# A two-layer graph network on one core: the edge load of a group of layer 0 is cut into four

## The reference, cut to what matters

```python
e = edge_attr @ W_edge + b_edge                  # 200000 x 128 times 128 x 256
msg = jax.nn.relu(x[src] + e)                    # gather of x rows by the edge's source
agg = jax.ops.segment_sum(msg, dst, num_segments=x.shape[0])
h = (1.0 + eps) * x + agg
h = jax.nn.relu(h @ W1 + b1) @ W2 + b2           # then a norm over the nodes, relu, residual, layernorm
```

## Time and profile before

| what | value |
|---|---|
| median of 3 timed runs | 5319.87 us (5314.68 to 5321.25) |
| profiled execution, its own time | 5282.99 us |
| its span from the first to the last instruction | 5281.1 us |
| layer 0's adds, first and last start | 34.71 us and 2505.15 us |
| mean granted TensorE clock | 0.828 of full speed |

### The profile page before, as it was taken

How to read it: one execution, slowest core, us unless ns; L and a number is a source line. 1 busy time by engine, 2 the same in 40 slices (tenths; PEclk the granted TensorE clock), 3 DMA queues, 4 the chain that set the end, 5 groups by cost and what they waited for, 6 DMA issues and landing times.

```text
span 5281.1 us, 64039 instructions
## 1 busy us (share of the span) xinstructions
PE 4024.7 (76%) x19280; PEld 2795.1 (53%) x19281; DVE 2232.9 (42%) x4481; ACT 719.6 (14%) x1302; POOL 3042.7 (58%) x3229
## 2 busy tenths in 40 slices
PE   6778778878777787777677777777777777777777
PEld 4566556556565565555444444444444444444444
DVE  4333333333333333233544444545455455555555
ACT  2211112221211221112300000000000000001101
POOL 6666656665655565554555555555555555555553
PEclk9888888988888888888877777778777777778877
DMA  4444444444443443432544444444444444444443
GB/s 149 134 129 133 134 127 132 129 139 126 131 123 115 128 130 117 124 117 87 150 116 121 122 122 121 121 122 119 121 116 123 121 121 119 121 116 121 119 120 86
DMA packets 321270, 650.08 MB, mean 123 GB/s; under 512 B 149823, under 2 KB 170537, under 8 KB 321225
## 3 DMA queue, kind: packets, MB, share of 16 engines
q0 software_dynamic: 150272, 413.00, 28.0%
q1 hardware_dynamic: 164681, 230.37, 13.3%
q10 hardware_dynamic: 6272, 6.19, 0.4%
HBM read 636.22 MB, written 13.08 MB: 123 GB/s over the span
## 4 chain that ended last, share of the span: by engine, by line
another core or an unknown queue 33%; PE 20%; issue 19%; DVEq 13%; DVE 12%; ACT 2%; ACTq 1%; DMA 0%; SPq 0%; POOLq 0%
PE psum L994 7%; PE psum L1005 5%; DVEq L818 3%; DVE rows L929 3%; DVE hot_t L850 3%; DVEq L1148 3%; PE psum L991 2%; DVEq L855 2%; PE psum L683 2%; DVE rows L1132 2%; DVEq L859 2%; PE psum L1033 1%; DVEq L1143 1%; PE psum L685 1%
## 5 line engine op out<-in xcount | busy, mean ns | idle before, releaser
L407 POOL DMA_INDIRECT rows<-z_tab,idx x1568 | 1514.5, 966 | 1127.3 <-DVEq L859 668.2
L407 POOL DMA_INDIRECT rows<-in_x,idx x1568 | 1490.8, 951 | 996.2 <-issue 454.2
L683 PE MATMUL psum<-onehot,rows 128*128 128x128 f32 x6272 | 1407.7, 359 | 576.5 <-DVEq L859 501.0
L683 PEld LDWEIGHTS psum<-onehot,rows 128*128 128x128 f32 x6272 | 1052.4, 239 | 1005.1 <-issue 1004.5
L1132 DVE TENSOR_TENSOR rows<-rows,psum 128x1024 f32<-128x1024 f32 x392 | 475.8, 1221 | 1688.3 <-remote 1051.4
L994 PE MATMUL psum<-weights,edge_room 128*128 128x256 f32 x3136 | 916.8, 417 | 37.8 <-issue 37.3
L1005 PE MATMUL psum<-rows,onehot 128*128 128x256 f32 x3136 | 845.2, 407 | 111.3 <-issue 108.9
L994 PEld LDWEIGHTS psum<-weights,edge_room 128*128 128x128 f32 x3136 | 664.9, 212 | 227.1 <-issue 72.1
L1005 PEld LDWEIGHTS psum<-rows,onehot 128*128 128x128 f32 x3136 | 624.6, 206 | 228.8 <-issue 149.1
L685 PE MATMUL psum<-onehot,rows 128*4 128x128 f32 x3136 | 704.6, 313 | 18.3 <-issue 18.3
L1078 ACT ACTIVATE rows<-rows 128x1024 f32<-128x1024 f32 x392 | 414.6, 1058 | 1957.7 <-DVE rows L1132 1369.8
(11 more groups left out here) (152 smaller groups left out, 1450.7 us busy)
## 6 DMA issues: line engine op xcount, KB each, us to landing
dst_t<-in_dst_jp SPq DMA_DIRECT2D x197, 512.0 KB
edge_room<-in_edge_t SPq DMA_DIRECT2D x196, 512.0 KB
rows<-in_x,idx POOLq DMA_INDIRECT x1568
rows<-z_tab,idx POOLq DMA_INDIRECT x1568
z_tab<-edge_room SPq DMA_DIRECT2D x14, 455.0 KB, 6.9
idx<-in_src_idx SPq DMA_DIRECT2D x392, 4.0 KB
dst_t<-in_x_t SPq DMA_DIRECT2D x14, 448.0 KB
rows<-in_x_t SPq DMA_DIRECT2D x14, 448.0 KB, 5.3
```

Source lines behind the costliest of these rows:

```text
L407: nc.gpsimd.indirect_dma_start(rows[0:count, u, j, 0:width], None, table, bass.IndirectOffsetOnAxis(ap=idx[0:count, u, j:j + 1], axis=0)). ...
L683: pe.matmul(banks[4 + k][:, 0:WIN], rows[:, u, j, k * P:(k + 1) * P], hot, start=(j == 0), stop=(j == J - 1))
```

## The change

SP's one edge load of 512 KB for a group becomes four loads of 128 KB (256 of the 1024 elements of each partition), and each waits for a count of its own. The first waits for what the whole load waited for. The second and the fourth wait for DVE's `added`, the third for PE's next `half_done`. PE's wait ahead of the first product of a group now asks for four loads' worth of counts.

```diff
                 sp.wait_ge(half_done, 2 * (g - RING) + 2)
-                sp.dma_start(edge_in[:, u, :], t["edge_t"][g]).then_inc(layer0.edge_in[u], 16)
+                for q in range(PAIRS):
+                    if q % 2 == 1:
+                        sp.wait_ge(added, 2 * (g - RING) + 2 + q)
+                        sp.sem_inc(passed, 1)
+                    elif q == 2:
+                        sp.wait_ge(half_done, 2 * (g - RING) + 4)
+                        sp.sem_inc(passed, 1)
+                    part = slice(2 * q * P, 2 * (q + 1) * P)
+                    sp.dma_start(edge_in[:, u, part], t["edge_t"][g, :, part]).then_inc(layer0.edge_in[u], 16)
             c0 = rounds(sp, body, load_nodes)
...
                 if b == 0:
-                    pe.wait_ge(layer0.edge_in[u], 16 * i + 16)
+                    pe.wait_ge(layer0.edge_in[u], 16 * PAIRS * i + 16)
```

## The result

The changed kernel took 5380.85 us, the median of 7 runs (5340.9 to 5401.5), beside 5321.25 us for the kernel before on the same chip (7 runs). The ratio is 1.0098, with a 95% interval of 1.0072 to 1.0125. It is 60 us slower, where no change was forecast (5319 us), and the median lies 31 us above the upper end of the range. The same pair, run again later beside a kernel before of 5273.03 us (chip 7), gave 1.0191 (1.0161 to 1.0221).

A forecast was written before the change was run, and what follows sets the result against it. Layer 0 was taken to be paced by PE's late counts, with no load waited for. Every term was priced at nothing, summing to 0 us on the profiled 5283 us; timed forecast 5319 us, eight in ten within 5280 to 5350 us.

The forecast's parts named there:

- the index load behind it: SP's 4 KB index load, queued behind the last quarter: at least 9.7 us from release to need; cost nothing.
- that x load: Load of x on SP, read 39 us after leaving; released up to 25 us later, 14 us remain; cost nothing.
- A margin is gone somewhere: Slower rival: index or x load needs over 9.7 us from release to landing; 196 us at 1 us a group; chance 0.02.
- The rival of the colliding quarters: Slower rival: last quarters fall among POOL's gathers, 0.46 us each in 95 waits; 5363 or 5341 us; chance 0.21.
- The faster rival: Edge-load bursts make PE's counts late; saving part of POOL's wait gives 5289 or 5242 us; chance 0.28.
- Smaller pieces, more DMAs: Per group, 1 KB pieces add 0.1 us of DMA time, three more DMAs 1.6 us on idle SP; cost nothing.
- POOL's "remote": Sign: POOL's layer 0 waits for "remote", 275 us in 84 waits, keep their sum within a tenth.
- DVE's 921 us: Sign: DVE's adds in layer 0 wait 921 us for "remote"; forecast wrong if this moves by more than 5%.
- Its gap ahead of a group: Sign: POOL's gap before a group's gathers, 4.05 us; forecast wrong if it takes another length.
- The quarters spread: SP issues three quarters after a first-half add, one after the next second-half product: 384 KB and 128 KB instead of 512 KB.
- I can't see why they are late: In layer 0, PE's count comes 11.7 us after the product's recorded end; the prediction left the cause unexplained.

The follow-up runs named there:

- e9: The changed kernel itself, run again beside the kernel before on chip 7: 5371.52 us, ratio 1.0191.
- e10: The changed kernel with the index load of group g+1 issued ahead of the quarters of group g, against the kernel before: 5290.34 us, ratio 1.0046.
- e11: The kernel before with its whole edge load released as late as the change's last quarter, index load issued ahead of it: 5357.65 us, ratio 1.0163.
- e1: The change's four 128 KB loads, all issued where the kernel before issues its one load, against that kernel: 5333.95 us, ratio 1.0007.
- e8: The kernel before without the edge loads of groups 4 to 195, the first four groups' edges read again: 4102.14 us, ratio 0.9999.
- e16: The kernel before without the edge loads of groups 4 to 195, run again: 4095.80 us, ratio 0.9999.
- e13: The kernel before with the wait of the change's last quarter set behind its one edge load: 4098.31 us, ratio 1.0.
- e14: The change without its last quarter's wait for an addition, so it leaves with the third, against the kernel before: 4093.67 us, ratio 0.9996.
- e6: The kernel before with only the index load issued later, behind its edge load and a wait for an addition: 4102.79 us, ratio 1.0001.

## Why the prediction was wrong

**The step that failed** is "the index load behind it", with its floor: "group A+5 can't want its indices sooner than 10.0 + 0.87 - 1.22 = 9.7 us after the count that releases SP. Cost nothing." The 9.7 us are right to 0.1 us in the changed kernel, and in ordinary groups they are enough: the median from index issue to gather is 10.3 us there, the least 6.9 us. But I read them against the landing of 4 KB only, in a stretch without a node step. At a node step SP has the load of x and the register work of the chunk's end to do between the last quarter and the next indices. These rows of the changed kernel show the slowest kind of such a step, SP and then POOL:

```profile
1189.23 0.33 SPq L978 DMA_DIRECT2D edge_room<-in_edge_t  x1
1195.68 0.69 SPq L962 DMA_DIRECT2D dst_t<-in_x_t  x1
1203.87 0.35 SPq L968 DMA_DIRECT2D idx<-in_src_idx  x1
```

```profile
1206.27 0.95 POOL L407 DMA_INDIRECT rows<-in_x,idx  x1 [5.90 <-DMA idx<-in_src_idx]
```

From the last quarter to the indices it is 14.6 us, with 9.7 to spend. Four of the 13 steps are like this (14.5 to 15.1 us, groups 96, 132, 160 and 180); in the other nine the walk takes 3.8 to 7.0 us, and the indices are in time. In the kernel before, the same walk (edge load 1139.88, x load 1142.66, indices 1145.25 us) took 5.4 us, and no index load left less than 19.2 us ahead of its gather. I had that x load in front of me, and priced its own margin, not what stood behind it. What the step priced at nothing cost 81 us of the 98 us on chip 7 (e9 against e10).

**The rival was named, and mis-sized.** "A margin is gone somewhere: index load or x load behind a count that comes late" had 0.02, and 1 us for every group. It happens at node steps only, and in e9 it costs more than the wait: a step is long (31.0 us in the mean of e9) or short (18.1 us), some 13 us apart, and 7 of its 8 steps with late indices are long. 10 long steps in place of 4 give 6 x 13 = 78 us, which is e9 less e10. That a late index makes a step long is read from these two profiles, and the others limit it: in the first result's profile all four steps with late indices are short, and e11 has 12 long steps with none. A late index is thus neither enough for a long step nor needed for one; the two gather groups that close up are what all long steps share. In the profiled run of the first result the share of the steps is also smaller: 29 of 65 us. The other 37 us are 0.2 us for each ordinary group, and I cannot say that they belong to the change: e1, which loses nothing in the timed runs, has 12.10 us for an ordinary group, and what follows layer 0's last addition, with code that is the same, was 32 us longer in the first pair (2808.1 against 2776.0 us). The run of before that I had lies 0.7% under its median.

**The rival of the colliding quarters** (0.21, 5341 or 5363 us) lay near in time, but its cause is not borne out: e9 and e10 move the same quarters at the same releases and differ by 81 us. It may hold part of the 17 us that e10 keeps (1.0046, 1.0023 to 1.007), and e11, a whole load at the late release with its indices in time, loses 85 us by something; whether that is a collision, no run tells.

**The faster rival** did not happen. No run with edge loads elsewhere, or with none, was clearly faster than the kernel before. But the two runs without edge loads (e8, e16) met no late counts, so the rival's own claim, that the bursts make the counts late, was not tested.

**Smaller pieces, more DMAs: "nothing"** was right (e1). The advice of the Trainium skill's page "DMA: Bandwidth & Descriptors", section "Bandwidth", to batch transfers to 1 MiB or more, which it gives beside loads issued from GpSimd, would have spoken against the quarters; here the four 128 KB loads, issued from SP, show no price (1.0007, 0.9986 to 1.0029).

**What would show it.** PE has no wait for the edges in the changed kernel, and POOL's "remote" kept within a tenth. DVE's 921 us moved by 10%, past the 5% that I had set. POOL has waits for indices, where I said none. Its gap ahead of a group, 4.05 us, took another length more often: of the groups 20 to 195, 55 have one of 2 to 3 us where the kernel before has 17. e1 has 47 of them at no loss, so this sign did not tell of one. The quarters spread, but not mainly as I wrote, three and then one. In 35 of 191 groups of the changed kernel the third quarter leaves more than 2 us behind such a three; in 75 it leaves with them, since the count that it waits for has come by then. The four quarters of one group leave within 3 us of each other in only 6 of 192 groups (the row of 2.32 us in e9 is one of 8 there).

**"I can't see why they are late", and going on,** was the deeper fault. Where these late counts are missing, every variant that ran there takes the same time: the change with the indices ahead 1.0006 (0.9997 to 1.0015), the wait of its last quarter alone 1.0, 0.9999 and 1.0002. The change itself was not among them, so that its loss hangs on the late counts is likely and not shown. I had half of the rule in a bracket, "2.9 us after POOL's last gather ended", and used it to price a collision instead of asking what happens to a node step when two groups of gathers close up.

**What stays open.** Why the late whole load makes nearly every node step long with the indices in time (e11, 85 us), I don't know; its ordinary groups are short (11.84 us). Nor do I know why the late indices of the first profile go with short steps. e13 and e14 would say whether the last quarter's wait is enough by itself and needed; they met no late counts. That the order on SP costs 81 us is shown by e10, on one chip; on the first result's 60 us no run settles the share. That the slow SP work at the chunk's end is the reason is read from timelines, not shown by an edit.

## What to carry to other kernels

A queue of loads on one engine is only as early as its latest wait: before moving a release, list everything that stands behind it on that engine, at the loop's rare places (ends of chunks, outer loops) as well as in its steady round, and compare the sum of their times with the margin. A mean over a layer hides two levels; split it by kind of step first. And where a wait in the profile can't be explained, its explanation may decide the sign of the change, and may not be there on the next occasion.

## What was not expected of the hardware

- One program, two speeds: 5273 to 5326 us on three occasions (chips 6, 7 and the first, whose number is not on record) and 4096 to 4103 us on four (chips 0, 1 and twice 4), with 0.82 to 0.83 and 0.95 to 0.96 of TensorE's clock granted over most executions. In layer 0 it is 0.87 from 250 to 2450 us before, that is 2.4 GHz with stretches at 1.2 GHz, and 0.99 from 250 to 1950 us in e6. The quick ones show no waits for "remote" there. No chip was met at both speeds, but most only once, so that it is the chip is not shown, nor whether the lower clock is a cause or a consequence.
- Where counts of PE are late, they arrive about 3 us after POOL's last gather (2.98 us in e9's step, 11.7 us after the recorded end of the products). POOL itself keeps its 1.25 us for a gather through it, while SP takes 9.4 us from the x load to the next indices in e9 and 2.6 us in the kernel before (1142.66 to 1145.25 us), and PE's matmuls in e9 start 1.4 to 2.1 us apart from 1511.3 to 1519 us in place of 0.22 us. It looks as if something that SP and PE need and POOL does not is held up; what it is, no run here shows.
- Edge traffic is free in this kernel where counts are not late: with 192 loads of 512 KB left out the ratio is 0.9999 (0.999 to 1.0008 in e8, 0.9991 to 1.0008 in e16).
